# Moving the second norm's statistics to ScalarE, one more head to VectorE, and reordering the routing tiles of a gated cross-attention and expert kernel

## The reference

```python
kv = (ctx @ W_kv.T + b_kv)          # k and v: 16 heads x 16 channels
q  = layernorm(x)                   # 16 heads
# for every token: scores between its own 16 heads, softmax, weighted sum of v
a  = softmax(einsum('bshd,bstd->bsht', q, k) / 4)
x  = x + tanh(g_xattn) * (einsum('bsht,bstd->bshd', a, v) @ W_out.T + b_out)
xn = layernorm(x)
p  = softmax(xn @ gate_w.T)         # 8 experts
g, m = top_k(p over tokens, 64)     # each expert of each batch takes 64 tokens
h  = gelu(xn[m] @ w1[e]) @ w2[e]    # 256 -> 1024 -> 256
x  = x + tanh(g_ffn) * scatter_add(m, g * h)
```

## Time and profile before

| | us |
|---|---|
| median of 3 runs (762.25 to 764.85) | 764.04 |
| the profiled execution, its own time | 766.51 |
| its span (first to last instruction) | 764.5 |
| busy: PE / DVE / POOL / ACT | 647.5 / 630.2 / 579.4 / 388.3 |

### The profile page before, as it was taken

One profiled execution on the slowest core, in us unless ns is written; L12 is line 12 of the kernel. 1 busy time (PEld: TensorE's weight loads), 2 busy tenths in 40 slices (PEclk: granted clock), 3 DMA queues, 4 the chain that ended last, 5 costly groups with the idle time before them and its releaser, 6 DMA issues.

```text
span 764.5 us, 10848 instructions
## 1 busy us (share of the span) xinstructions
PE 647.5 (85%) x3592; PEld 517.6 (68%) x3592; DVE 630.2 (82%) x894; ACT 388.3 (51%) x882; POOL 579.4 (76%) x497
## 2 busy tenths in 40 slices
PE   5678867453689999984999999859999999999994
PEld 2234433221478888873878888747888889999994
DVE  5899999997999999967999999859999743567672
ACT  5466656432466666733666666535665542323321
POOL 3899989996877999867898889858899833445443
PEclk9877898755699999996999999977999999999998
DMA  6877755230347878764688887536777878899982
GB/s 192 311 237 252 263 203 200 103 132 27 111 152 222 244 231 244 214 182 126 189 243 253 247 232 226 186 89 191 233 225 220 238 227 281 286 306 317 304 252 27
DMA packets 97069, 160.91 MB, mean 210 GB/s; under 512 B 8171, under 2 KB 74486, under 8 KB 97014
## 3 DMA queue, kind: packets, MB, share of 16 engines
q1 hardware_dynamic: 84150, 142.91, 56.1%
q0 software_dynamic: 12288, 16.79, 11.6%
q10 hardware_dynamic: 576, 0.52, 0.2%
HBM read 126.63 MB, written 33.55 MB: 210 GB/s over the span
## 4 chain that ended last, share of the span: by engine, by line
PE 55%; POOL 19%; DVE 8%; DMA 7%; issue 7%; ACT 3%; POOLq 0%; ACTq 0%; DVEq 0%
PE bank L1010 20%; PE bank L991 20%; POOL prod_p L313 9%; DMA out_dram<-ys,ids 7%; POOL tree_a L319 5%; PE bank L918 4%; DVE prod_v L456 3%; PE bank L938 3%; POOL tree_b L319 3%; PE bank L901 2%; PE bank L979 2%; POOL tree_c L319 1%; DVE co L458 1%; PE bank L950 1%; PE bank L927 1%
## 5 line engine op out<-in xcount | busy, mean ns | idle before, releaser
L991 PE MATMUL bank<-xin,w1in 128*128 128x256 f32 x1536 | 210.3, 296 | 5.5 <-DVE xin L592 3.8
L991 PEld LDWEIGHTS bank<-xin,w1in 128*128 128x128 f32 x1536 | 199.5, 202 | 7.2 <-issue 6.8
L1010 PE MATMUL bank<-w2s,hT 128*128 128x256 f32 x768 | 175.4, 382 | 0.0
L379 POOL DMA_INDIRECT out_dram<-ys,ids x64 | 110.0, 1719 | 75.6 <-ACT ys L747 57.9
L1010 PEld LDWEIGHTS bank<-w2s,hT 128*128 128x128 f32 x768 | 142.4, 190 | 17.7
L737 ACT ACTIVATE hT<-bank 128x512 f32<-128x512 f32 x128 | 76.4, 597 | 118.5 <-PE bank L991 118.1
L313 POOL TENSOR_TENSOR prod_p<-kvs,q 128x1024 f32<-128x1024 f32 (+2 forms) x32 | 99.8, 3118 | 13.0 <-ACT q L704 12.9
L458 DVE TENSOR_REDUCE co<-prod_v 128x192 f32<-128x3072 f32 (+1 forms) x32 | 104.6, 3270 | 1.1
L456 DVE TENSOR_TENSOR prod_v<-bank,Ex 128x3072 f32<-128x3072 f32 (+1 forms) x32 | 104.5, 3265 | 0.1
L456 DVE TENSOR_TENSOR prod_v<-bank,q 128x3072 f32<-128x3072 f32 (+2 forms) x32 | 95.5, 2983 | 6.3 <-ACT q L704 6.3
L365 POOL DMA_INDIRECT xg<-xn_scratch,ids x64 | 65.0, 1016 | 46.1 <-DVE ids L582 28.6
(11 more groups left out here) (118 smaller groups left out, 1044.9 us busy)
## 6 DMA issues: line engine op xcount, KB each, us to landing
w1in<-w_parts SPq DMA_DIRECT2D x128, 512.0 KB, 5.4
w2s<-in_L_ffn_w_dram SPq DMA_DIRECT2D x32, 1024.0 KB, 6.2
w_parts<-w1s SPq DMA_DIRECT2D x32, 512.0 KB, 3.4
w1raw<-in_L_ffn_w_dram SPq DMA_DIRECT2D x32, 256.0 KB, 4.3
ct<-in_ctx_dram SPq DMA_DIRECT2D x32, 128.0 KB, 5.3
xt<-in_x_dram SPq DMA_DIRECT2D x32, 128.0 KB, 4.2
out_dram<-x SPq DMA_DIRECT2D x32, 128.0 KB, 4.2
xn_scratch<-xn SPq DMA_DIRECT2D x32, 128.0 KB, 2.7
```

The source lines that it names most:

```text
L379: pool.indirect_dma_start(out=out_rows[:, :], out_offset=bass.IndirectOffsetOnAxis(ap=ids[:, g % 2, p * E + e:p * E + e + 1], axis=0), in_ ...
L991: ins = pe.matmul(HB[k % 2][:, D * f:D * (f + 1)], w1in[:, k, w, c, P * f:P * (f + 1)].bitcast(f32r), xin[:, n % 2, x_, c, :], start=(m == ...
L1010: ins = pe.matmul(dst, hT[:, n % 2, f, cols], w2s[:, n % 2, f, :], start=(f == 0), stop=(f == FC - 1))
```

## The change

- VectorE's `stats` goes. ScalarE's `x2_stats` takes its place with five instructions like those of `x_stats`: sum, mean, squares with their sum, variance. It stands at the end of the step in tiles 0 to 9; between `make_q` and `take_y` (before `gate_exp`) in ordinary tiles from 11 on; after `exponentials` and `take_y` in routing tiles; and before the last `make_xn`.
- EARLY becomes (11, 11), LATE (12, 13).
- In routing tiles GpSimd does `rsqrt(s+1)` ahead of `scores(s)`; VectorE does `residual(s-1)` ahead of `routes`; TensorE does the probability transposes ahead of the hidden products and `route_columns` ahead of the second half of the outputs; ScalarE warms Exp and does the exponentials right after `make_q`, and `take_y` after them.
- The eighth round of the choice leaves out match_replace.

```diff
-    EARLY, LATE, ROUTING = (10, 11), (12, 12), (4, 12)
+    EARLY, LATE, ROUTING = (11, 11), (12, 13), (4, 12)
...
             for s in range(NT):
+                if routing(s):
+                    rsqrt(s + 1)
                 scores(s)
-                rsqrt(s + 1)
+                if not routing(s):
+                    rsqrt(s + 1)
...
-                if t > 0 and not routing(t):
+                if t > 0:
                     residual(t - 1)
                 if routing(t):
                     routes(t // TG - 1)
...
-                if t > 0 and routing(t):
-                    residual(t - 1)
-                if t > 0:
-                    stats(t - 1)
...
-                    dve.max_index(top_i[:, eight], top_p[:, eight], work[:, :])
-                    dve.match_replace(work[:, :], top_p[:, eight], work[:, :], -1.0).then_inc(removed8, 1)
-                    wait_apart(removed8, n + 1)
+                    if r < CAP // 8 - 1:
+                        dve.max_index(top_i[:, eight], top_p[:, eight], work[:, :])
+                        dve.match_replace(work[:, :], top_p[:, eight], work[:, :], -1.0).then_inc(round_done, 1)
+                    else:
+                        dve.max_index(top_i[:, eight], top_p[:, eight], work[:, :]).then_inc(round_done, 1)
+                    wait_apart(round_done, n + 1)
...
+            def x2_stats(t):
+                act.wait_ge(x2_ready, t + 1)
+                act.activation(x_junk[:, :], x2[:, t % 2, :], ACT.Copy, accum_out=x2_sum[:, :]).then_inc(x2_step, 1)
+                act.wait_ge(x2_step, 3 * t + 1)
+                act.activation(x2_mean[:, t % 2:t % 2 + 1], x2_sum[:, :], ACT.Copy, scale=-1.0 / D).then_inc(x2_step, 1)
+                act.wait_ge(x2_step, 3 * t + 2)
+                act.activation(x_junk[:, :], x2[:, t % 2, :], ACT.Square, bias=x2_mean[:, t % 2:t % 2 + 1],
+                               accum_out=x2_square[:, :]).then_inc(x2_step, 1)
+                act.wait_ge(x2_step, 3 * t + 3)
+                act.wait_ge(rs_ready, t + 3)
+                act.activation(ve[:, 1:2], x2_square[:, :], ACT.Identity, bias=eps[:, :], scale=1.0 / D).then_inc(ve_ready, 1)
...
                 take_ctT(s + 2)
+                if s >= 1:
+                    x2_stats(s - 1)
...
+                if routing(s):
+                    if n >= 0:
+                        take_ctT(s + 1)
+                        gelu(n, 0)
+                        gelu(n, 1)
+                    take_coT(s - 1)
+                    take_kv(s + 1)
+                    make_xn(s - 2)
+                    x_stats(s + 2)
+                    take_xnT(s - 2)
+                    if n >= 0:
+                        gelu(n, 2)
+                        gelu(n, 3)
+                    take_logits(s - 2)
+                    make_q(s + 1)
+                    act.activation(exp_warm[:, :], tanh_g[:, 0:1], ACT.Exp)
+                    exponentials(s)
+                    if n >= 1:
+                        take_y(n - 1)
+                    x2_stats(s - 1)
+                    take_xh(n + 1)
+                    continue
...
+            for s in range(N0 - 1, NT):
+                n = s - N0
+                if n >= 0 and s + 1 < NT:
+                    ctx_transposes(s + 1)
+                if routing(s):
+                    prob_transposes(s // TG - 1)
+                if n >= 0:
+                    hidden(n, 0)
+                    hidden(n, 1)
+                co_transposes(s - 1)
...
+                logits(s - 2)
+                if routing(s):
                     route_columns(s // TG - 1)
+                if n >= 1:
+                    outputs(n - 1, 1)
+                if routing(s):
                     token_transposes(n + 1)
```

More of the change, by code:

```diff
@@ L114, in flamingo_gated_block_kernel @@
         exp_warm = sb("exp_warm", [P, 1])
-        st2 = sb("st2", [P, 6])
-        mv2 = sb("mv2", [P, 2])
+        x2_sum = sb("x2_sum", [P, 1])
+        x2_square = sb("x2_square", [P, 1])
         x2_mean = sb("x2_mean", [P, 2])
@@ L814, in _ @@
                 n = s - N0
-                if n >= 0 and s + 1 < NT:
-                    take_ctT(s + 1)
-                if 0 <= n < NE:
-                    gelu(n, 0)
-                    gelu(n, 1)
-                if 0 < s <= NT:
-                    take_coT(s - 1)
-                if n >= 0 and s < NT and not routing(s):
-                    act.activation(exp_warm[:, :], tanh_g[:, 0:1], ACT.Exp)
+                if routing(s):
[20 more added lines that the diff above has]
+                    continue
@@ L824, in _ @@
+                if s + 1 < NT:
+                    take_ctT(s + 1)
+                gelu(n, 0)
+                gelu(n, 1)
+                take_coT(s - 1)
+                act.activation(exp_warm[:, :], tanh_g[:, 0:1], ACT.Exp)
                 if s + 1 < NT:
                     take_kv(s + 1)
-                if s < NT and not routing(s):
-                    exponentials(s)
-                if 0 <= n + 1 < NE and not routing(s):
-                    take_xh(n + 1)
-                if s <= NT + 1:
-                    make_xn(s - 2)
@@ L832, in _ @@
-                if n >= 0:
-                    if s + 2 < NT:
-                        x_stats(s + 2)
-                    if s <= NT + 1:
-                        take_xnT(s - 2)
-                if 0 <= n < NE:
-                    gelu(n, 2)
-                    gelu(n, 3)
-                if routing(s) and 0 <= n - 1 < NE:
-                    take_y(n - 1)
-                if s >= 2 and n < 0:
-                    take_xnT(s - 2)
-                if s <= NT + 1:
-                    take_logits(s - 2)
@@ L846, in _ @@
-                if s + 2 < NT and n < 0:
+                exponentials(s)
+                take_xh(n + 1)
+                make_xn(s - 2)
+                if s + 2 < NT:
                     x_stats(s + 2)
+                take_xnT(s - 2)
+                gelu(n, 2)
+                gelu(n, 3)
+                take_logits(s - 2)
                 if s + 1 < NT:
                     make_q(s + 1)
-                if routing(s + 1) and s <= NT + 1:
+                x2_stats(s - 1)
+                if routing(s + 1):
@@ L851, in _ @@
                     gate_exp(s // TG - 1)
-                if s < NT and routing(s):
-                    exponentials(s)
-                if 0 <= n + 1 < NE and routing(s):
-                    take_xh(n + 1)
-                if 0 <= n - 1 < NE and not routing(s):
+                if n >= 1:
                     take_y(n - 1)
@@ L864, in _ @@
             take_xnT(NT - 2)
+            x2_stats(NT - 1)
             make_xn(NT - 1)
@@ L1045, in _ @@
             pe.wait_ge(minus_ready, 1)
[L1046 to L1071 removed]
+            for s in range(N0 - 1):
+                if s > 0:
+                    co_transposes(s - 1)
+                project_kv(s + 1)
+                if s > 0:
+                    project_out(s - 1)
                 if s < E:
```

76 lines of the change are left out of this document (21 added, 55 removed).

## The result

The changed kernel takes **736.95 us** (median of 4 runs, 736.47 to 738.09) and the kernel before, run beside it, 764.44 (4 runs, 762.25 to 767.35). The ratio is 0.964, with a 95% interval of 0.9605 to 0.9675: faster by 3.6%, 27.5 us. The forecast was 735.7, with a range of 731 to 742. The profiled execution took 736.63, its span is 734.6, so against the span before of 764.5 it has 29.9 less. That is 2.4 more than the medians differ, because the profiled execution of before was a long one (766.51).

The account below looks back on a forecast made before the run. It took GpSimd to bound tiles 0 to 9, TensorE ordinary tiles from 11, and chains of waits the routing tiles. Gains 5.3 + 6.6 + 8.2 + 8.2 = 28.3 from the 764.04 median gave 735.7 us, range 731 to 742.

Parts of the forecast that it names:

- Early tiles: Tiles 0 to 9, head added to VectorE, statistics off it: 4.2 for nine periods, 1.1 for tile 0; 5.3 us.
- Ordinary tiles: Tiles from 11 on: TensorE stays full at 17.65 us, gain 0; loss of 1.7 each if ScalarE's statistics are uncovered.
- Tile 10: Routing tile without hidden product: den 5.3 earlier, plus 1.32 from residual and statistics; gain 6.6 us.
- Tiles 18 and 26: Routing tiles with hidden products: exponentials 6.85 earlier, residual and statistics 1.32 out of the way; gain 8.2 us each.
- Steps 1 to 5: Tile 18: early rsqrt, 1.6 wait for pr, earlier ids, no wait for xn, den 6.85 us earlier.
- One slack: Tile 18: gather rows 2.9 us after issue, tokens copied by 346.6, 2.3 before low_tokens.
- A: Tiles 18 and 26: TensorE loses its clock at the wait for pr; 739.1 to 740.9 us; chance 0.11.
- C: Routing step: GpSimd becomes the bound, con and scores late, three times up to 3 us; 737 to 745; chance 0.10.
- B: Hidden product after routing tiles: clock returns sooner, three times 0.9 us; 733; chance 0.10.
- D: Early tiles: the head move buys nothing, the period stays 15.22; 741 us; chance 0.04.
- E: Tiles 18 and 26: pr or a load holds TensorE as xn did, leaving only 1.32 each; 749.5 us; chance 0.04.
- F: Ordinary tiles from 11: ScalarE's statistics displace take_y, ctT and Gelus; slower from 1.5 us each, 774 at 2.0; chance 0.03.

Follow-up runs that it names:

- experiment 3: Changed kernel with EARLY back at (10, 11), GpSimd doing six heads of scores in tiles 0 to 9: 743.72 us.
- Experiment 11: Changed kernel with ScalarE computing the statistics a second time, into an unread spare tile, in each step from 11 on: 740.53 us.
- experiment 1: order_only: new routing-tile order and shorter last round, against the kernel before; statistics stay on VectorE, heads (10, 11), (12, 12): 743.6 us.
- 6: Changed kernel with GpSimd's rsqrt behind its scores again in routing tiles: 742.03 us.
- experiment 8: Changed kernel with statistics before the second pair of Gelus ahead of routing steps, and exponentials ahead of make_q in tiles 18 and 26: 733.51 us.
- experiment 5: Changed kernel with TensorE's old order in routing tiles, hidden products ahead of probability transposes, second outputs ahead of route matmuls: 740.7 us.
- experiments 8 to 10: Experiment 8 (733.51 us), then two built on it: routing-tile gather ahead of both additions of results (735.77 us), or between them (732.57 us).
- stats_only: Kernel before with only the statistics moved to ScalarE; old heads, old order, old eighth round: 758.99 us.

## Why the prediction was right

**Early tiles.** Right in mechanism and size: 4.1 for nine periods, period 14.75, VectorE without a wait; experiment 3 shows that the head is its cause. That the statistics had to leave VectorE first is an estimate from the forecast's own terms: with them, the head would make VectorE's cycle 15.03 + 0.53 = 15.56, longer than the 15.22 before. No run has the head with the statistics on VectorE. Tile 0, counted from its first product (13.82 before, 14.17 after), gave 1.0 of 1.1.

**Ordinary tiles.** Right: 0. Experiment 11 shows the cover to be wider than the rows of before told. That Square needs no load behind a Gelu stands in the timeline above. The Trainium skill, ScalarE: Activation LUTs, section Table sets, doesn't list Square for that set; the trace, with no load beside it in 19 ordinary tiles, says more than the page does.

**Tile 10.** 6.6 forecast, 6.6 measured. By experiment 1 the order has 5.0 of it, by 6 rsqrt first 2.6 of that.

**Tiles 18 and 26.** 8.2 forecast each, 8.45 and 9.2 measured. Steps 1 to 5 are there one by one: rsqrt ahead of the product, a wait for pr of 1.37 instead of 1.6, no wait for xn, exponentials after 16.3 instead of 16.0. Up to the start of the next hidden product it is 8.1 and 8.0, and the surplus lies behind it; in tile 26 0.9 of it is clock, since that product took 4.53 instead of 5.46.

One slack was mis-sized. I had the gather's rows 2.9 after issue, as before; in tile 18 they came 5.5 after it (327.58 to 333.1), in tile 26 4.2. In tile 18 the tokens' copy was ready at 334.96, so 0.5 before xin began and not 2.3. It cost nothing here, but made experiment 8 fall short. The forecast had counted the loads and the store that now go out earlier as free, because nobody waits for them. What it didn't ask is what they do to the gather. Windows from its issue to its rows, before and after (columns as in the earlier trace rows), and SyncE's load of w2 in the changed kernel:

```profile
346.30:349.10 2.80, 0.00 (x0) 0.00 (x0) 0.72 (x4) 2.24 (x3) 2.44 (x3) 1.00 0.16 47
```

```profile
327.58:333.00 5.42, 1.99 (x10) 1.40 (x8) 4.55 (x3) 3.10 (x11) 5.03 (x4) 1.00 0.95 244
```

```profile
329.60 0.38 SPq L229 DMA_DIRECT2D w2s<-in_L_ffn_w_dram  x1
```

Before, the gather had the DMA engines nearly to itself (busy share 0.16); the load of w2 went out at 356.60, long after. Now they are full (0.95). Two kinds of transfer are in it: the additions, right ahead of the gather now and 7.3 us ahead of it before, and those of SyncE (loads of w1, the store of the residual, the load of w2). With the gather first its rows came 4.0 and 3.9 after issue, with it between the additions 5.1 and 4.2, right behind both 4.2 to 5.5. The additions alone don't explain it: in experiment 5 they stand where they stood, the gather is 1.0 further behind them, and its rows took 7.3, with the load of w2 now ahead of it. Which transfer slows it by how much was not isolated.

**What the sum didn't have.** Behind tile 10, 2.1 were won where I had 0, and at the end 1.1 lost. The second hidden product of step 11 and the first of step 12, before and after (timelines of TensorE; the product at 209.24 stands behind the wait of 1.50 in the earlier trace rows):

```profile
209.24 3.12 PE L991 MATMUL bank<-xin,w1in 128*128 128x256 f32 x24
...
215.95 4.60 PE L991 MATMUL bank<-xin,w1in 128*128 128x256 f32 x24 [2.97 <-DVE xin L592]
```

```profile
197.35 0.44 PE L908 MATMUL bank<-ident,xn 128*128 128x128 f32 x2 [1.50 <-ACT xn L715]
197.55 4.61 PE L998 MATMUL bank<-xin,w1in 128*128 128x256 f32 x24
...
204.00 3.11 PE L998 MATMUL bank<-xin,w1in 128*128 128x256 f32 x24 [1.23 <-issue]
```

Both kernels have one slow product here, with nearly the same lost in it. In the changed kernel it is the earlier one, and it runs while VectorE is still making the next tokens, so that TensorE then idles 1.23 instead of 2.97. These 1.7 are most of the 2.1. Which product is the slow one follows no edit: the idle time before the earlier one is 1.50 in all thirteen kernels, and it was the earlier one that took 4.61 in four of them (stretch 24.14 to 24.66), the later one in eight (25.37 to 26.60, the kernel before among them) and both in order_only (26.25).

And the last 28 to 30 us, before and after (windows; the last but two number is the granted clock):

```profile
736.00:764.50 28.50, 18.68 (x152) 18.10 (x150) 11.80 (x16) 4.91 (x10) 11.68 (x6) 0.92 0.40 85
```

```profile
705.00:734.60 29.60, 19.84 (x152) 19.47 (x150) 11.79 (x16) 4.92 (x10) 11.67 (x6) 0.88 0.38 78
```

At the end it is clock: 0.88 over that stretch instead of 0.92, so that the same 152 products took 19.84 instead of 18.68. Neither is the change's own with any certainty. The first stretch is 24.54 here, 24.66 with the statistics before the Gelus, and 25.73 to 25.82 in the three kernels of experiments 8 to 10, none of which touches it. Some 0.8 of the 2.1 is left even in those three, against the one trace of before. The last is 88.1 to 89.8 over all kernels, with no pattern by edit, and den of tile 0 lies between 20.93 and 22.69 in those with the changed kernel's heads. Each of these spreads is as large as the 1.3 us by which 735.7 missed.

**The rivals.** A did not come: behind 1.37 idle the product took 3.12 in both tiles. But the forecast's reason against it was no reason. It held 1.50 of idle time for safe because of one row, and in the changed kernel's own step 11 the product behind just such a wait took 4.61, while in experiment 11 one behind 2.96 took 3.11. The length of the wait doesn't tell, and the record has no better account; that A stayed away was in part luck. Its upper price was too high as well: by the earlier trace rows a product wholly at half clock costs 5.46 - 3.11 = 2.35 more, not 2.6. B came in part, in one tile of two (4.53, but 5.41). C did not come: con was not late. D is out by experiment 3, E and F by the trace, F by experiment 11 too.

## What to carry to other kernels

Work added to an engine that waits in every tile costs nothing there, but look for the one step in which something else stands behind it: here it brought a wait of 1.4 us in each of two routing tiles, and the same instructions two Gelus earlier took it away. The worth of an edit depends on what else was changed. The statistics moved off VectorE bought 6.0 us alone, nothing on top of the new order, and were, by estimate, what made room for the head's 6.8; that the two halves run alone make 27.3 of 27.5 must not be read as a sum. And rsqrt first looked worth 12 to 14 us by the rows of the kernel before and was worth 5 in the finished one. Where the next engine is right behind the leading one, measure what a transfer or a queue does once it is issued sooner; its latency from the old place does not carry over, and a load that nobody waits for can still slow a transfer that somebody does.

## What the runs showed of the hardware

- The length of an idle time did not tell whether TensorE kept its full clock. Behind 1.37 the product of 24 matmuls took 3.11 to 3.12 in eight cases of eight. Behind the 1.50 of step 11 it took 3.11 to 3.12 in eight kernels and 4.60 to 4.61 in five. In stats_only a wait of 2.55 was followed by 4.62 in tile 18 and by 3.11 in tile 26; in experiment 11 two waits of 2.96 were followed by 3.11 and 3.12; in the kernel before one of 2.97 was followed by 4.60.
- A gather of the same size had its rows 2.9 us after issue with the DMA engines at a busy share of 0.16, 5.5 with them at 0.95, and 7.3 with both additions and a load of 1 MB issued ahead of it.
